# Causal attention between two expert layers: scores in sets of three heads over three PSUM banks, two sets in turn, and a probability ring of five

## The chip, the cores and the metric

The kernel runs on one NeuronCore of one Trainium2 chip. The metric is the device time of one execution in microseconds (us); the kernel before was timed three times.

## The reference

The input x has 2 sequences of 1024 tokens with 128 features. Three layers follow each other, each added to x: half of an expert layer, causal attention, and half of the same expert layer again.

```python
x = x + 0.5 * ffn(layernorm(x))     # 8 experts, 128 -> 256 -> 128, gelu, all summed, one gate value per token
x = x + attention(layernorm(x))     # 8 heads of 8 features
x = x + 0.5 * ffn(layernorm(x))
...
q, k = l2norm(q), l2norm(k)
sim = einsum('bhid,bhjd->bhij', q, k) * 8.0
attn = softmax(where(causal_mask, sim, finfo.min))
o = einsum('bhij,bhjd->bhid', attn, v) @ w_out
```

## The kernel before, in words

The program is written engine by engine. Each engine runs its own list in order, and every dependence is a semaphore: `scores_done`, `exp_done`, `mask_done` and `pv_done` count the four stages of attention.

**Expert layers.** Tokens go in four groups of 512; a group has 16 chunks of 128 hidden rows. A chunk is three matmuls up (`up`, L455), a gelu on ACT (L782), a split into a high and a low part on DVE (`split`, L949) and three matmuls down (`down`, L479). Attention lies between the last group of the first layer and the first group of the second.

**Attention.** The 8 heads form two quads of four. A pair is one sequence `b` and one group of 512 queries `qg`, with both quads; there are four pairs. A unit is one pair and one quad (L218). For each unit, `score_items` (L90) lists items: one per key block of 128 keys before the diagonal, then three for the four diagonal blocks, packed as 512 columns, 384 + 128 columns, and 256 columns. A unit with `qg` 0 has 3 items, one with `qg` 1 has 7. Before the change a whole unit is done before the next, so its sibling quad comes after it.

A step is one item of two heads; 80 steps make 40 quad steps. For a step:

- PE writes the scores of two heads into two banks of PSUM (`scores`, L592). Banks 0 to 5 form three sets (`S_SETS` = 3, `score_set`, L251), so scores of step s wait for the exponential of step s - 3 (`set_reader`, L255).
- ACT takes one exponential over both banks (`exp_scores`, L797) into a ring of 8 buffers (`P_SLOTS`). It waits for the probability product that last read the buffer.
- GpSimd (POOL) zeroes what lies above the diagonal with `affine_select` (L1305 to L1313), 128x256 elements each.
- PE multiplies the probabilities of four heads with v (`pv`, L606), in f32, into one output bank per pair (7 or 6 in turn), a row of 32 partitions per head.

The order on PE is written out at L685 to L713: for quad step k the two score sets, then `pv(k - 3)` (`PV_LAG` = 3), then perhaps one job.

Jobs (L242, `fill` L631 on PE, `empty` L1137 on DVE) use the other output bank: the layernorm transposes of the last token group ("ln"), its q, k, v product in two halves ("qkv"), the transposes of stacked q and k ("q_stack", "k_stack"), the output projection of a finished pair in two halves ("project") and the transposes for the second expert layer ("ffn_ln"). Each names the quad step whose `pv` it follows, counted from q1, q2, q3, the first quad steps of pairs 1 to 3. A job waits until DVE has emptied the job before it, and the first `pv` of pairs 2 and 3 waits for all jobs before it, since its output bank was the job bank.

```python
for k in range(quad_steps + PV_LAG):
    ...
        for s in (2 * k, 2 * k + 1):
            ...
            scores(s)
    ...
    if k >= PV_LAG:
        ...
        pv(k - PV_LAG)
        if jobs[next_job][0] == k - PV_LAG:
            fill(next_job)
```

Some steps are scored early, inside the last token group of the first expert layer (L537 to L557): steps 0 to 3, two on banks 0 and 1 and two on banks 2 and 3.

Of the kernel before, what the change touches and what calls it, by code (L numbers as in the profile page):

```python
# [48 lines left out]
QUADS = 2  # L49
ROW = 32  # L50
# [6 lines left out]
S_SETS = 3  # L57
P_SLOTS = 8
PV_LAG = 3
FFN, ATT = 0, 1  # L60
# [38 lines left out]
def build(nc, x, ln_w, ln_b, w_qkv, w_out, gate_w, gate_b, rms_w, w1, b1, w2, b2, out):  # L99
# [9 lines left out]
    with ctx:  # L109
        def sb(name, shape, dt=f32):  # L110
            return ctx.enter_context(nc.sbuf_tensor(name, shape, dt))
# [59 lines left out]
        probs = sb("probs", [P, P_SLOTS, 2, GROUP])  # L171
# [47 lines left out]
        steps = []  # L219
        for u, (b, qg, quad) in enumerate(units):  # L220
            items = score_items(qg)
            for k, item in enumerate(items):
                for pair in range(2):
                    steps.append(dict(unit=u, b=b, qg=qg, quad=quad, pair=pair, item=item, first=(k == 0),
                                      last=(k == len(items) - 1), local=k,
                                      diagonal=any(kt >= GROUP_TILES * qg for kt, *_ in item)))
        masks_until, n_masks = [], 0
        for st in steps:
            n_masks += len(st["item"]) if st["diagonal"] else 0
            masks_until.append(n_masks)  # L230
        quad_steps = len(steps) // 2
        quads_until_unit = [max(i for i, st in enumerate(steps) if st["unit"] == u) // 2 + 1 for u in range(len(units))]
        last_quad = [n - 1 for n in quads_until_unit]
# [5 lines left out]
        pairs = len(units) // QUADS  # L239
        first_of_pair = [0] + [quads_until_unit[QUADS * i - 1] for i in range(1, pairs)]  # L240
# [3 lines left out]
                (q1 + 12, "q_stack", LAST), (q2 + 1, "k_stack", LAST),  # L244
# [5 lines left out]

        def score_set(s):  # L251

            return s % 2 if s < 4 else (s - 2) % S_SETS

        def set_reader(s):  # L255

            return s - 2 if s in (2, 3) else None if s == 4 or s < 2 else s - S_SETS

        def output_bank(pair):
            return 7 - pair % 2  # L260

        def job_bank(n):

            at = jobs[n][0]
            return 13 - output_bank(steps[2 * min(at, quad_steps - 1)]["unit"] // QUADS)

        def pair_of_job(n):
            return steps[2 * min(jobs[n][0], quad_steps - 1)]["unit"] // QUADS
# [161 lines left out]
        def _(pe):  # L430
# [77 lines left out]
            def ffn_group(layer, g):  # L508
# [5 lines left out]
                for c in range(CHUNKS):  # L514
# [39 lines left out]
                    if operands and last and c >= at["att_qkv"]:  # L554
# [37 lines left out]
            def scores(s):  # L592
                st = steps[s]
                if set_reader(s) is not None:
                    pe.wait_ge(exp_done, set_reader(s) + 1)
                for kt, q0, width, at in st["item"]:
                    k0 = SEQ * st["b"] + P * kt
                    qc = SEQ * st["b"] + GROUP * st["qg"] + q0
                    for hd in range(2):
                        j = 2 * st["pair"] + hd  # L600
                        rows = slice(ROW * j, ROW * j + ROW)
                        m = pe.matmul(ps[:, 2 * score_set(s) + hd, at:at + width], kT[rows, st["quad"], k0:k0 + P],  # L602
                                      qT[rows, st["quad"], qc:qc + width], start=True, stop=True)
                m.then_inc(scores_done, 1)

            def pv(k):  # L606

                s = 2 * k
                st = steps[s]
                pair = st["unit"] // QUADS  # L610
                bank = output_bank(pair)
                opens, closes = st["first"] and st["quad"] == 0, st["last"] and st["quad"] == QUADS - 1
                if opens and pair == 0:
                    pe.wait_ge(kT_done, LAST - 1)
                if opens and pair == 1:
                    pe.wait_ge(resid, GROUP_TILES * GROUPS)
                if opens and pair > 1:
                    pe.wait_ge(job_emptied, sum(at < k for at, *_ in jobs))
                if st["diagonal"]:
                    pe.wait_ge(mask_done, masks_until[s + 1])  # L620
                else:
                    pe.wait_ge(exp_done, s + 2)
                for n, (kt, q0, width, at) in enumerate(st["item"]):
                    for j in range(4):
                        m = pe.matmul(ps[ROW * j:ROW * j + ROW, bank, q0:q0 + width],  # L625
                                      v_ones[:, SEQ // P * st["b"] + kt, 4 * st["quad"] + j, :],
                                      probs[:, (s + j // 2) % P_SLOTS, j % 2, at:at + width],
                                      start=(opens and n == 0), stop=(closes and n == len(st["item"]) - 1))
                m.then_inc(pv_done, 1)
# [54 lines left out]
            next_job = 0  # L684
            for k in range(quad_steps + PV_LAG):  # L685
                if k < quad_steps:
                    st = steps[2 * k]
                    if st["first"]:
                        p = Q_GROUPS * st["b"] + st["qg"]
                        if p < GROUPS // 2:  # L690
                            pe.wait_ge(kT_done, p + 1)
                        else:
                            pe.wait_ge(job_emptied, job_number["k_stack", p] + 1)
                    for s in (2 * k, 2 * k + 1):
                        if s < 4:
                            continue
                        if s == 4:
                            pe.wait_ge(qkv_copied, LAST)
                            pe.wait_ge(y_evac, GROUPS)
                            pe.wait_ge(xf_done[FFN], GROUPS)  # L700
                        scores(s)
                    if k == 0:
                        y_transposes(LAST, BANK_YT_LAST)
                if k >= PV_LAG:
                    if k == quad_steps + PV_LAG - 1:
# [20 lines left out]
        def _(act):  # L726
# [70 lines left out]
            def exp_scores(s):  # L797
                act.wait_ge(scores_done, s + 1)
# [76 lines left out]
            for s in range(2, len(steps)):  # L875
                exp_scores(s)
# [6 lines left out]
        def _(dve):  # L883
# [234 lines left out]
            def output(pair):  # L1118

                dve.wait_ge(pv_done, quads_until_unit[QUADS * pair + QUADS - 1])  # L1120
# [108 lines left out]
        def _(pool):  # L1229
# [75 lines left out]
            for s, st in enumerate(steps):  # L1305
                if not st["diagonal"]:
                    continue
                pool.wait_ge(exp_done, s + 1)

                for _, _, _, at in st["item"]:  # L1310
                    region = probs[:, s % P_SLOTS, :, at:at + P]
                    pool.affine_select(region, region, [[0, 2], [1, P]], ALU.is_ge, 0.0, base=0,  # L1312
                                       channel_multiplier=-1).then_inc(mask_done, 1)  # L1313
                if s == 5:
                    ln_twice(LAST)
                if s == 2 * last_quad[3] + 1:
                    ln_once(GROUPS)
# [20 lines left out]
```

## Time and profile before

| what | value |
|---|---|
| median of 3 runs | 288.85 us (288.41 to 289.15) |
| the profiled execution | 288.67 us, its span 286.9 us |
| PE busy | 274.2 us, 96% of the span |
| ACT busy | 222.8 us, 78% |
| DVE busy | 216.9 us, 76% |
| POOL busy | 87.6 us, 31% |
| granted TensorE clock, mean | 0.999 |

The span runs from the first to the last instruction; the execution's time holds 1.8 us more around it. Busy time of an engine is an average over stages: in the expert layers PE is busy throughout, while in attention, from 119 to 185 us, ACT has work almost all the time. A record of an operation may overlap the next, on PE and on ACT, so the pace of an engine is read from start to start, not from the length of a record. Where an engine idles, the page names the engine that ended the wait.

### The profile page before, as it was taken

The numbers are of one execution on the slowest core, as the hardware profiler recorded it, in microseconds if no ns is written. First come the engines' busy times: TensorE is split into PE (matmuls) and PEld (weight loads), VectorE is DVE, ScalarE is ACT, GpSimd is POOL, SyncE is SP. The second block draws the span as 40 slices with busy tenths as digits, with TensorE's granted clock in tenths as the row PEclk, the third lists the DMA queues.
The fourth block names the chain that finished last, engine by engine and source line by source line (L and its number), as shares of the span: only waits on it lengthen the run. The fifth ranks groups of instructions, "written<-read, shape, count | busy, mean of one in ns | idle before, by whom it ended". The sixth has DMA issues, their size and how long they took to land.

```text
span 286.9 us, 5191 instructions
## 1 busy us (share of the span) xinstructions
PE 274.2 (96%) x1651; PEld 191.6 (67%) x1651; DVE 216.9 (76%) x573; ACT 222.8 (78%) x346; POOL 87.6 (31%) x155
## 2 busy tenths in 40 slices
PE   8998999999989998899998999999999999999994
PEld 8675788788778886432433432378888888888882
DVE  7699989888989889855588153078788898797765
ACT  2766876868787785999999999976785877677672
POOL 6326203301890383361438321401300310310010
PEclk9999999999999999999999999999999999999999
DMA  5720000000000000000000000000001000100101
GB/s 156 233 73 1 0 1 2 0 0 1 2 1 0 3 1 0 0 2 2 0 3 0 3 0 2 0 2 0 0 2 39 0 0 0 37 0 2 38 0 37
DMA packets 8107, 4.64 MB, mean 16 GB/s; under 512 B 690, under 2 KB 8084, under 8 KB 8084
## 3 DMA queue, kind: packets, MB, share of 16 engines
q1 hardware_dynamic: 8084, 4.35, 5.3%
q8 instruction: 12, 0.20, 0.3%
q14 instruction: 11, 0.09, 0.1%
HBM read 3.30 MB, written 1.05 MB: 15 GB/s over the span
## 4 chain that ended last, share of the span: by engine, by line
PE 73%; POOL 8%; ACT 8%; issue 5%; DVE 4%; DVEq 0%; POOLq 0%; ACTq 0%
PE ps L494 9%; PE ps L489 9%; PE ps L471 8%; PE ps L477 8%; PE ps L474 8%; PE ps L492 8%; PE ps L625 8%; ACT probs L803 5%; PE ps L602 3%; PE ps L664 2%; PE ps L656 2%; PE ps L451 2%; PE ps L580 2%; PE ps L442 2%; POOL rstd L1231 1%
## 5 line engine op out<-in xcount | busy, mean ns | idle before, releaser
L790 ACT ACTIVATE h<-ps,cols 128x512 f32<-128x512 f32 x128 | 87.9, 691 | 48.8 <-PE ps L477 43.5
L958 DVE TENSOR_TENSOR h_lo<-h,h_hi 128x512 fp32r<-128x512 f32 x128 | 92.0, 724 | 29.6 <-ACT h_hi L793 27.1
L803 ACT ACTIVATE probs<-ps 128x1024 f32<-128x1024 f32 (+1 forms) x80 | 67.0, 1013 | 0.6 <-PE ps L602 0.4
L489 PE MATMUL ps<-h_hi,w_hi 128*128 128x512 f32 x128 | 52.9, 413 | 0.3 <-DVE h_hi L956 0.3
L494 PE MATMUL ps<-h_lo,w_hi 128*128 128x512 f32 x128 | 50.9, 398 | 1.4 <-DVE h_lo L958 1.4
L471 PE MATMUL ps<-xT_hi,w_hi 128*128 128x512 f32 (+1 forms) x128 | 50.7, 396 | 0.1
L477 PE MATMUL ps<-xT_lo,w_hi 128*128 128x512 f32 (+1 forms) x128 | 50.0, 391 | 0.0
L492 PE MATMUL ps<-h_hi,w_lo 128*128 128x512 f32 x128 | 50.0, 391 | 0.0
L474 PE MATMUL ps<-xT_hi,w_lo 128*128 128x512 f32 (+1 forms) x128 | 49.9, 389 | 0.0
L793 ACT ACTIVATE h_hi<-ps,cols 128x512 fp32r<-128x512 f32 x72 | 49.2, 683 | 0.0
L1312 POOL TENSOR_SCALAR_AFFINE_SELECT probs<-probs 128x256 f32<-128x256 f32 x64 | 26.0, 431 | 46.5 <-ACT probs L803 46.0
L625 PE MATMUL ps<-probs,v_ones 128*32 128x512 f32 (+3 forms) x384 | 38.8, 495 | 0.0
L494 PEld LDWEIGHTS ps<-h_lo,w_hi 128*128 128x128 f32 x128 | 24.0, 188 | 9.5 <-DVE h_lo L958 4.4
L956 DVE CAST h_hi<-h 128x512 fp32r<-128x512 f32 x56 | 24.9, 444 | 7.0 <-ACT h L790 6.2
L489 PEld LDWEIGHTS ps<-h_hi,w_hi 128*128 128x128 f32 x128 | 24.1, 188 | 5.8 <-DVE h_hi L956 1.6
L471 PEld LDWEIGHTS ps<-xT_hi,w_hi 128*128 128x128 f32 x128 | 24.0, 188 | 5.6 <-ACT h L790 0.4
L477 PEld LDWEIGHTS ps<-xT_lo,w_hi 128*128 128x128 f32 x128 | 24.0, 188 | 5.5 <-DVE xT_lo L1182 0.2
L474 PEld LDWEIGHTS ps<-xT_hi,w_lo 128*128 128x128 f32 x128 | 24.0, 188 | 5.1
L492 PEld LDWEIGHTS ps<-h_hi,w_lo 128*128 128x128 f32 x128 | 24.1, 189 | 3.9
L602 PE MATMUL ps<-qT,kT 32*128 32x512 f16 (+3 forms) x192 | 21.3, 329 | 2.9 <-ACT probs L803 2.3
L602 PEld LDWEIGHTS ps<-qT,kT 32*128 32x128 f16 x192 | 6.5, 91 | 25.2 <-ACT probs L803 15.1
L1231 POOL TENSOR_TENSOR gate_rms<-gate_ms,neg_half 128x4 f32<-128x4 f32 x8 | 10.6, 1320 | 28.5 <-DVE gate_ms L923 28.5
(130 smaller groups left out, 288.4 us busy)
## 6 DMA issues: line engine op xcount, KB each, us to landing
w_raw<-in_L_ffn_w SPq DMA_DIRECT2D x8, 256.0 KB, 4.9
x_sb<-in_L_attn_x SPq DMA_DIRECT2D x3, 256.0 KB, 6.8
out_x<-x_sb SPq DMA_DIRECT2D x3, 256.0 KB, 2.3
x_sb<-in_L_attn_x SPq DMA_DIRECT2D x2, 128.0 KB, 2.2
out_x<-x_sb SPq DMA_DIRECT2D x2, 128.0 KB, 1.8
wout_sb<-in_L_attn_w_out SPq DMA_DIRECT2D x8, 4.0 KB
wqkv_sb<-in_L_attn_w_qkv SPq DMA_DIRECT2D x1, 96.0 KB, 6.0
small<-in_L_ffn_b SPq DMA_DIRECT2D x1, 8.0 KB
```

Of the source, the lines that this page charges most:

```text
L471: pe.matmul(bank, w1_hi[:, w], xT_hi[:, cols_g], start=True, stop=False)
L474: pe.matmul(bank, w1_lo[:, w], xT_hi[:, cols_g], start=False, stop=False)
L477: pe.matmul(bank, w1_hi[:, w], xT_lo[:, cols_g], start=False, stop=True).then_inc(up_done, 1)
L489: pe.matmul(y, w2_hi[:, w], h_hi[:, c % RING, :], start=(c == 0), stop=False)
L492: pe.matmul(y, w2_lo[:, w], h_hi[:, c % RING, :], start=False, stop=False)
L494: pe.matmul(y, w2_hi[:, w], h_lo[:, c % RING, :], start=False, stop=(c == CHUNKS - 1)).then_inc(down_done, 1)
L602: m = pe.matmul(ps[:, 2 * score_set(s) + hd, at:at + width], kT[rows, st["quad"], k0:k0 + P], qT[rows, st["quad"], qc:qc + width], start=T ...
L625: m = pe.matmul(ps[ROW * j:ROW * j + ROW, bank, q0:q0 + width], v_ones[:, SEQ // P * st["b"] + kt, 4 * st["quad"] + j, :], probs[:, (s + j ...
L790: first = nc.scalar.activation(h[:, slot, :], ps[:, BANK_H + slot, :], ACT.Gelu, bias=bias)
L793: nc.scalar.activation(h_hi[:, slot, :], ps[:, BANK_H + slot, :], ACT.Gelu, bias=bias).then_inc(gelu_done, 1)
L803: nc.scalar.activation(probs[:, s % P_SLOTS, :, 0:width], ps[:, bank:bank + 2, 0:width], ACT.Exp, scale=SCALE).then_inc(exp_done, 1)
L958: dve.tensor_tensor(h_lo[:, slot, :], h[:, slot, :], h_hi[:, slot, :].bitcast(f32), ALU.subtract).then_inc(split_done, 1)
```

## The change

Slots take the place of steps of two heads. A slot is 512 columns of scores of one head; the 256-column items of both quads share a slot, so all 144 slots are full. The pairs go key block by key block, both quads of a key block after each other (`steps` is now one entry for four heads of one quad). Slots are cut into sets: three early sets of two, 45 sets of three, then two and one, 50 in all. From the fourth on a set has banks 0 to 2 or 3 to 5 in turn, so that scores of set n wait for the exponential of set n - 2. One exponential covers the whole set, up to 128x1536. The ring has five sets (`P_SETS`); the exponential of set n waits for all `pv` that read set n - 5. A `pv` comes on PE in the turn of set (its last set + 3), or + 4 where it is masked, after that set's scores. Masks take up to three slots at once. The job "k_stack" of the last group moves from the second quad step of pair 2 to the last of pair 1. Only three sets are scored early.

```diff
-S_SETS = 3
-P_SLOTS = 8
-PV_LAG = 3
+SET = 3
+P_SETS = 5
+EARLY_SETS = 3
+PV_LAG, PV_LAG_MASKED = 3, 4
...
+        sizes = [2] * EARLY_SETS
+        sizes += [SET] * ((len(slots) - sum(sizes)) // SET - 1) + [2, 1]
...
+        def set_bank(n):
+            return 2 * (n % 2) if n < EARLY_SETS else SET * (n % 2)
...
+        turn_of_step = [last_set[k] + (PV_LAG_MASKED if st["diagonal"] else PV_LAG) for k, st in enumerate(steps)]
+        turn_of_step = [max(turn_of_step[:k + 1]) for k in range(quad_steps)]
...
-                (q1 + 12, "q_stack", LAST), (q2 + 1, "k_stack", LAST),
+                (q1 + 12, "q_stack", LAST), (q1 + 13, "k_stack", LAST),
...
-            def scores(s):
-                st = steps[s]
-                if set_reader(s) is not None:
-                    pe.wait_ge(exp_done, set_reader(s) + 1)
+            def scores(n):
+                if banks_free_after(n):
+                    pe.wait_ge(exp_done, banks_free_after(n))
...
+            for n in range(EARLY_SETS, max(turn_of_step) + 1):
...
+                    scores(n)
+                while next_step < quad_steps and turn_of_step[next_step] == n:
+                    if next_step == quad_steps - QUADS:
+                        pe.wait_ge(exp_done, len(sizes) - 1)
                         for c in range(LAG):
-                            pe.wait_ge(exp_done, len(steps) - 2 + c // 2 + 1)
                             up(1, GROUPS, c, 0)
-                    pv(k - PV_LAG)
-                    if jobs[next_job][0] == k - PV_LAG:
+                    pv(next_step)
+                    if jobs[next_job][0] == next_step:
                         fill(next_job)
                         next_job += 1
+                    next_step += 1
...
-                if s >= P_SLOTS:
-                    act.wait_ge(pv_done, (s - P_SLOTS) // 2 + 1)
-                width = sum(w for _, _, w, _ in steps[s]["item"])
-                bank = 2 * score_set(s)
-                nc.scalar.activation(probs[:, s % P_SLOTS, :, 0:width], ps[:, bank:bank + 2, 0:width], ACT.Exp,
+                if n >= P_SETS:
+                    act.wait_ge(pv_done, max(steps_reading(n - P_SETS)) + 1)
+                bank = set_bank(n)
+                nc.scalar.activation(probs[:, n % P_SETS, 0:sizes[n], :], ps[:, bank:bank + sizes[n], :], ACT.Exp,
                                      scale=SCALE).then_inc(exp_done, 1)
```

The diff decides the order by these tables, so here is what PE's list becomes at two places. In it `ps<-qT,kT` is scores, `ps<-probs,v_ones` is `pv`, and `ps<-ident,q_stack` and `k_stack` are jobs. First PE where attention takes over, after the transposes of the last expert output; before, scores of steps 4 to 7 and then the first `pv`:

```order
L602 MATMUL ps<-qT,kT 128x256 [waits xf_done_ffn,y_evac,qkv_copied]
L602 MATMUL ps<-qT,kT 128x256
L602 MATMUL ps<-qT,kT 128x256 [waits exp_done]
L602 MATMUL ps<-qT,kT 128x256
L602 MATMUL ps<-qT,kT 128x512 [waits exp_done,kT_done]
L602 MATMUL ps<-qT,kT 128x512
L602 MATMUL ps<-qT,kT 128x512 [waits exp_done]
L602 MATMUL ps<-qT,kT 128x512
L625 MATMUL ps<-probs,v_ones 32x512 [waits mask_done,kT_done]
L625 MATMUL ps<-probs,v_ones 32x512 x3
```

Now, scores of sets 3, 4 and 5 and then the first `pv`:

```order
L650 MATMUL ps<-qT,kT 128x512 [waits xf_done_ffn,exp_done,y_evac,qkv_copied]
L650 MATMUL ps<-qT,kT 128x512
L650 MATMUL ps<-qT,kT 128x384
L650 MATMUL ps<-qT,kT 128x128
L650 MATMUL ps<-qT,kT 128x384 [waits exp_done]
L650 MATMUL ps<-qT,kT 128x384 x2
L650 MATMUL ps<-qT,kT 128x128 x3
L650 MATMUL ps<-qT,kT 128x384 [waits exp_done]
L650 MATMUL ps<-qT,kT 128x384 x2
L650 MATMUL ps<-qT,kT 128x128 x3
L673 MATMUL ps<-probs,v_ones 32x512 [waits mask_done,kT_done]
L673 MATMUL ps<-probs,v_ones 32x512 x3
```

The first `pv` stands behind scores that wait for an exponential two sets earlier; the exponential of set 5 in turn reuses the probabilities' buffer of set 0, which this `pv` reads.

Second PE at the seam from pair 1 to pair 2. Before, the q transposes of the last group follow one `pv`, scores follow them, then the `pv` of 256 columns and scores again; the k transposes come three quad steps after the q transposes, behind these rows:

```order
L580 MATMUL ps<-ident,q_stack 128x128 [waits stack_done,job_emptied]
L580 MATMUL ps<-ident,q_stack 128x128 x7
L602 MATMUL ps<-qT,kT 128x256 [waits exp_done]
L602 MATMUL ps<-qT,kT 128x256
L602 MATMUL ps<-qT,kT 128x256 [waits exp_done]
L602 MATMUL ps<-qT,kT 128x256
L625 MATMUL ps<-probs,v_ones 32x256 [waits mask_done]
L625 MATMUL ps<-probs,v_ones 32x256 x3
L602 MATMUL ps<-qT,kT 128x512 [waits exp_done,job_emptied]
L602 MATMUL ps<-qT,kT 128x512
L602 MATMUL ps<-qT,kT 128x512 [waits exp_done]
L602 MATMUL ps<-qT,kT 128x512
```

Now the two short steps of pair 1, with one job each, stand behind the scores of one set (set 28):

```order
L650 MATMUL ps<-qT,kT 128x384 [waits exp_done]
L650 MATMUL ps<-qT,kT 128x384 x2
L650 MATMUL ps<-qT,kT 128x128 x3
L673 MATMUL ps<-probs,v_ones 32x256 [waits mask_done]
L673 MATMUL ps<-probs,v_ones 32x256 x3
L623 MATMUL ps<-ident,q_stack 128x128 [waits stack_done,job_emptied]
L623 MATMUL ps<-ident,q_stack 128x128 x7
L673 MATMUL ps<-probs,v_ones 32x256 [waits mask_done]
L673 MATMUL ps<-probs,v_ones 32x256 x3
L623 MATMUL ps<-ident,k_stack 128x128 [waits stack_done,job_emptied]
L623 MATMUL ps<-ident,k_stack 128x128 x7
```

What moved: both `pv` of 256 columns and both transpose jobs are in one turn, between the scores of set 28 and those of set 29, the next rows.

## Rows read from the trace of the kernel before

**Rows 1.** The page: busy time of each engine and share of the span.
```profile
PE 274.2 (96%) x1651; PEld 191.6 (67%) x1651; DVE 216.9 (76%) x573; ACT 222.8 (78%) x346; POOL 87.6 (31%) x155
```

**Rows 2.** Busy time by stretch, attention: us, PE, PEld, DVE, ACT, POOL, PEclk, DMA, GB/s.
```profile
132.00:146.00 14.00, 14.00 (x136) 5.43 (x128) 8.85 (x27) 13.85 (x17) 3.75 (x8) 1.00 0.01 1
...
119.00:185.00 66.00, 61.77 (x620) 21.59 (x624) 34.63 (x99) 65.40 (x80) 27.05 (x66) 1.00 0.01 1
```

**Rows 3.** Groups by line and shape, 115 to 190 us: the exponentials.
```profile
L803 ACT ACTIVATE probs<-ps 128x1024 f32<-128x1024 f32 x64 | 59.9, 1099 | 0.2
...
L803 ACT ACTIVATE probs<-ps 128x512 f32<-128x512 f32 x16 | 9.2, 668 | 0.4 <-PE ps L602 0.4
```

**Rows 4.** Timeline, ACT alone: start us, us, engine, line, what.
```profile
119.15 1.02 ACT L803 ACTIVATE probs<-ps 128x1024 f32<-128x1024 f32 x1
...
172.74 1.02 ACT L803 ACTIVATE probs<-ps 128x1024 f32<-128x1024 f32 x1
...
183.60 1.22 ACT L803 ACTIVATE probs<-ps 128x512 f32<-128x512 f32 x2
...
184.08 0.74 ACT L803 ACTIVATE probs<-ps 128x512 f32<-128x512 f32 x1
```

**Rows 5.** Timeline, PE: scores, probs times v, and jobs, back to back.
```profile
132.65 0.66 PE L647 MATMUL ps<-ident,xn 128*128 128x128 f32 x4
...
142.97 0.92 PE L650 MATMUL ps<-wqkv_sb,xf 128*128 128x192 f32 x4
...
143.82 0.40 PE L602 MATMUL ps<-qT,kT 32*128 32x512 f16 x4
...
144.14 1.07 PE L625 MATMUL ps<-probs,v_ones 128*32 128x512 f32 x8
...
145.14 0.62 PE L580 MATMUL ps<-ident,q_stack 128*128 128x128 f16 x8
...
145.69 0.40 PE L602 MATMUL ps<-qT,kT 32*128 32x512 f16 x4
...
154.63 0.29 PE L602 MATMUL ps<-qT,kT 32*128 32x256 f16 x4
...
154.85 0.64 PE L625 MATMUL ps<-probs,v_ones 128*32 128x256 f32 x8
...
162.98 0.71 PE L656 MATMUL ps<-wout_sb,o_feat 128*128 128x128 f32 x4
```

**Rows 6.** Timeline, PE: scores that ACT waits for, and scores that wait for ACT.
```profile
172.31 0.40 PE L602 MATMUL ps<-qT,kT 32*128 32x512 f16 x4
...
177.48 0.39 PE L602 MATMUL ps<-qT,kT 32*128 32x512 f16 x2 [0.47 <-ACT probs L803]
```

**Rows 7.** The chain that ended last, 171 to 186 us.
```profile
176.37 0.40 ACT probs L803
...
179.99 0.79 ACT probs L803
```

**Rows 8.** Timeline, DVE and PE: a job that waits, and one emptied.
```profile
153.32 0.62 DVE L378 TENSOR_TENSOR k_stack<-qkn,k_stack 128x256 f16<-128x256 f32 x1
...
154.09 0.61 PE L580 MATMUL ps<-ident,q_stack 128*128 128x128 f16 x8 [0.81 <-DVE k_stack L378]
...
163.72 0.42 DVE L1170 TENSOR_TENSOR x_sb<-ps,x_sb 128x256 f32<-128x256 f32 x1 [4.04 <-PE ps L656]
```

**Rows 9.** Timeline, POOL: masks.
```profile
171.75 1.48 POOL L1312 TENSOR_SCALAR_AFFINE_SELECT probs<-probs 128x256 f32<-128x256 f32 x4 [0.15 <-ACT probs L803]
...
181.16 0.41 POOL L1312 TENSOR_SCALAR_AFFINE_SELECT probs<-probs 128x256 f32<-128x256 f32 x1 [7.92 <-ACT probs L803]
```

**Rows 10.** Timeline, PE: start of the exponential stream and its end.
```profile
120.06 0.44 PE L602 MATMUL ps<-qT,kT 32*128 32x256 f16 x4
...
185.91 0.50 PE L471 MATMUL ps<-xT_hi,w_hi 128*128 128x512 f32 x1
...
188.75 0.50 PE L471 MATMUL ps<-xT_hi,w_hi 128*128 128x512 f32 x1
```

More of the change, by code:

```diff
@@ L218, in build @@
         units = [(b, qg, quad) for b in range(BATCH) for qg in range(Q_GROUPS) for quad in range(QUADS)]
-        steps = []
-        for u, (b, qg, quad) in enumerate(units):
+        pairs = len(units) // QUADS
+        slots, steps = [], []
+        for pair in range(pairs):
+            b, qg, _ = units[QUADS * pair]
             items = score_items(qg)
             for k, item in enumerate(items):
[L223 to L226, printed above, removed]
+                width = sum(w for _, _, w, _ in item)
+                together = width < GROUP
+                diagonal = any(kt >= GROUP_TILES * qg for kt, *_ in item)
+                first_slot = len(slots)
+                for quads in ([range(QUADS)] if together else [[quad] for quad in range(QUADS)]):
+                    for j in range(4):
+                        slots.append(dict(pair=pair, b=b, qg=qg, item=item, diagonal=diagonal, j=j, opens=(k == 0),
+                                          heads=[(quad, width * n) for n, quad in enumerate(quads)]))
+                for quad in range(QUADS):
+                    steps.append(dict(pair=pair, b=b, quad=quad, item=item, diagonal=diagonal,
+                                      slot=first_slot if together else first_slot + 4 * quad,
+                                      base=width * quad if together else 0,
+                                      opens=(k == 0 and quad == 0),
+                                      closes=(k == len(items) - 1 and quad == QUADS - 1)))
@@ new lines, in banks_free_after, with steps_reading, mask_regions @@
+        def banks_free_after(n):
+            mine = range(set_bank(n), set_bank(n) + sizes[n])
+            users = [m for m in range(n) if any(bank in mine for bank in range(set_bank(m), set_bank(m) + sizes[m]))]
+            return max(users) + 1 if users else 0
+        def steps_reading(n):
+            return [k for k, st in enumerate(steps) if any(set_of_slot[st["slot"] + j] == n for j in range(4))]
+        def mask_regions(n):
+            regions = []
+            for i, slot in enumerate(slots_of[n]):
+                if not slots[slot]["diagonal"]:
+                    continue
+                starts = sorted(at + base for _, base in slots[slot]["heads"] for *_, at in slots[slot]["item"])
+                if regions and regions[-1][2] == starts and regions[-1][1] == i:
+                    regions[-1][1] = i + 1
+                else:
+                    regions.append([i, i + 1, starts])
+            return regions
@@ L234, in build @@
+        turn_of_step = [last_set[k] + (PV_LAG_MASKED if st["diagonal"] else PV_LAG) for k, st in enumerate(steps)]
+        turn_of_step = [max(turn_of_step[:k + 1]) for k in range(quad_steps)]
+        steps_until_pair = [sum(st["pair"] <= pair for st in steps) for pair in range(pairs)]
+        last_mask_of_pair = [max(n for n in range(len(sizes)) if any(slots[i]["pair"] == pair and slots[i]["diagonal"] for i in slots_of[n]))
+                             for pair in range(pairs)]
         halves = ((0, 1), (2, 3))
@@ L235, in build @@
         SEED_OPS = 4
[L239 to L240 removed]
+        first_of_pair = [0] + steps_until_pair[:-1]
         q1, q2, q3 = first_of_pair[1:]
@@ L590, in stack_transposes @@
                 transpose_stack(k_stack, BANK_KT).then_inc(stack_t, 1)
-            def scores(s):
-                st = steps[s]
-                if set_reader(s) is not None:
-                    pe.wait_ge(exp_done, set_reader(s) + 1)
[L596 to L603, printed above, removed]
+            def scores(n):
+                if banks_free_after(n):
+                    pe.wait_ge(exp_done, banks_free_after(n))
+                parts = max(len(slots[i]["item"]) * len(slots[i]["heads"]) for i in slots_of[n])
+                for part in range(parts):
+                    for i in slots_of[n]:
+                        slot = slots[i]
+                        pieces = [(quad, base, piece) for quad, base in slot["heads"] for piece in slot["item"]]
+                        if part >= len(pieces):
+                            continue
+                        quad, base, (kt, q0, width, at) = pieces[part]
+                        k0 = SEQ * slot["b"] + P * kt
+                        qc = SEQ * slot["b"] + GROUP * slot["qg"] + q0
+                        rows = slice(ROW * slot["j"], ROW * slot["j"] + ROW)
+                        bank = set_bank(n) + i - first_slot[n]
+                        m = pe.matmul(ps[:, bank, base + at:base + at + width], kT[rows, quad, k0:k0 + P],
+                                      qT[rows, quad, qc:qc + width], start=True, stop=True)
@@ L604, in scores @@
                 m.then_inc(scores_done, 1)
             def pv(k):
-                s = 2 * k
-                st = steps[s]
-                pair = st["unit"] // QUADS
+                st = steps[k]
+                pair = st["pair"]
                 bank = output_bank(pair)
-                opens, closes = st["first"] and st["quad"] == 0, st["last"] and st["quad"] == QUADS - 1
-                if opens and pair == 0:
+                if st["opens"] and pair == 0:
                     pe.wait_ge(kT_done, LAST - 1)
-                if opens and pair == 1:
+                if st["opens"] and pair == 1:
@@ L683, in _ @@
             pe.wait_ge(wout_in, 16 * HEADS)
[L684 to L705, printed above, removed]
+            y_transposes(LAST, BANK_YT_LAST)
@@ L874, in _ @@
             ffn_groups(nc.scalar, 0, lambda g: ffn_group(0, g))
-            for s in range(2, len(steps)):
-                exp_scores(s)
+            for n in range(2, len(sizes)):
+                exp_scores(n)
             for c in range(LAG):
```

75 lines of the change are left out of this document (45 added, 30 removed).

## Prediction

> **What bounds the kernel now.** I read the page first, then the busy time by stretch, then the timeline of each engine inside attention. The page gives PE 96% of the span [rows 1], and the expert layers, which the change leaves alone, make that share. Attention is the stretch from 119 to 185 us: ACT is busy for 65.4 of 66.0 us, PE for 61.8 [rows 2]. Between 132 and 146 us PE is busy for all of 14.0 us [rows 2]. So the reader should see two engines that are both nearly full: ACT sets the pace, and PE has next to nothing to spare where jobs lie between the steps.
>
> ACT's own pace is read from starts. From 172.74 to 183.60 us twelve exponentials of 1024 columns begin, 0.905 us each; the last two, of 512 columns, begin 0.48 us apart [rows 4]. A column thus costs (0.905 - 0.48) / 512 = 0.83 ns and an instruction 0.055 us on top. There are 64 and 16 of them [rows 3]; two ran before 119.15 us. The rest need 62 x 0.905 + 15 x 0.48 = 63.3 us up to the start of the last, which came 64.9 us after 119.15 [rows 4]: ACT lost only 1.6 us to waits. The three sets of banks keep it fed.
>
> **What the change gives.** Columns stay the same: 144 slots of 512, or 64 x 1024 + 16 x 512. Instructions go from 80 to 50, which saves 30 x 0.055 = 1.65 us if ACT never waits. A set of 1536 columns should take 0.48 + 2 x 0.425 = 1.33 us; no row has that width, and I extend the line through the two that are there.
>
> The row leaves 0.055 us for an instruction. [...]
>
> **What it costs: the loop of two sets.** Steps on the loop, each from a row. Scores that wait for ACT start 1.11 us after the start of a 0.905 us exponential (176.37 [rows 7] to 177.48 [rows 6]), so 0.21 after its pace is over. Four heads' scores occupy PE for 0.33 us (145.69 to the next piece; 143.82 to 144.14 gives 0.32) [rows 5], and I take that for three. From the start of scores to the start of the waiting exponential is 0.43 (172.31 [rows 6] to 172.74 [rows 4]), so 0.10 for the signal. A `pv` of 512 columns takes 1.00 (144.14 to 145.14 [rows 5]); one of 256 takes 0.57, its record of 0.64 running 0.07 into the next as the others do [rows 5]. By the same reading jobs take 0.59 (ln), 0.85 (half of qkv), 0.55 (a stack) and 0.64 (half a projection) [rows 5]. Between a job's end and PE's next job DVE needs 0.10 to start, 0.42 to add (162.98 + 0.64 to 163.72) and 0.15 back to PE (153.94 to 154.09) [rows 5, 8], about 0.69.
>
> Call the start of exponential n - 2 zero. Exponential n is due at 2.66. Its banks are free at 1.33 + 0.21 = 1.54, its scores end at 1.87, ACT could go at 1.97. Before, the banks of step s were those of s - 3 and scores ran a set ahead. Now PE has, after the scores of set n, until 3.99 - 0.43 = 3.56 for all other work of that turn without hurting set n + 1: 1.69 us. One `pv` and a projection (1.64) just fit; more does not, and a second such turn has only 1.00.
>
> 1. *Start.* The third early set has banks 0 and 1, so set 3 needs banks that the last expert output holds. Its scores can start where those of step 4 now do, 120.06 [rows 10]; add 0.43: 120.49, against 119.15 + 0.905 = 120.05. Loss 0.44. Before, steps 2 and 3 covered this.
> 2. *The ring of five.* In masked stretches `pv` comes with a lag of four sets, so the exponential of set n waits for a `pv` that PE does after the scores of set n itself: 1.87 + 1.00 + 0.10 = 2.97 against 2.66, 0.30 each. A late set gives the next one room, so it is paid at about every second set. Going through the 50 sets with these numbers I find it at sets 5, 7, 10, 23, 26, 30, 32, 34 and 47: 9 x 0.30 = 2.70. After set 23 a stack job lies between, and set 24 pays 0.55.
> 3. *Seam of pairs 0 and 1* (turn 11): `pv` 0.57 + 0.57 + 1.00, ln 0.59 = 2.73, less 1.69, less 0.30 already late: 0.74.
> 4. *qkv jobs* (turns 18 and 19): 1.85 each, so 0.16, then 1.85 - 1.00 = 0.85, together 1.01.
> 5. *Projections* of pairs 0 and 2, two turns in a row: 2 x 1.64 - 1.69 - 1.00 = 0.59, less about 0.3 since the turn before them is empty: 2 x 0.3 = 0.6.
> 6. *Seam of pairs 1 and 2* (turn 28): exponential 28 waits for the second short `pv`, behind a stack: 1.87 + 0.57 + 0.55 + 0.57 + 0.10 = 3.66, loss 1.00. The second stack then waits for DVE in the shadow of that.
> 7. *Seam of pairs 2 and 3* (turn 35): exponential 35 waits for `pv` 0.57, projection 0.64, `pv` 0.57: 3.75 - 2.66 - 0.30 = 0.79. Then the second projection waits 0.12 for DVE and takes 0.64, the first `pv` of pair 3 waits 0.69 for its output bank and takes 1.00, and only then come the scores of set 36, 0.43: 2.88, less 0.10 and 1.33 that set 35 covers: 1.45.
>
> Sum of waits: 0.44 + 2.70 + 0.55 + 0.74 + 1.01 + 0.60 + 1.00 + 2.24 = 9.28 us, in place of 1.6.
>
> *The end.* Before, from the end of the last exponential's pace (184.08 + 0.48) to PE's free run into the second expert layer (188.75 [rows 10]) are 4.19 us. Now from the start of set 47: 1.33, POOL's start 0.27 (179.99 + 0.905 to 181.16 [rows 7, 9]), four masks of about 0.37 or less, 1.22 together [rows 9], about 0.2 back to PE (my estimate, beside the 0.15 from DVE), `pv` 1.0, three chunks up 2.27 (185.91 to 188.75 less a `pv` of 0.57 [rows 5, 10]), two short `pv` 1.14: 7.43, while ACT ends at 1.33 + 0.905 + 0.48 = 2.71. So 4.72, a loss of 0.53.
>
> Costed at nothing: the masks elsewhere (POOL is busy for 27 of 66 us [rows 2] and has four sets of time), and the moved "k_stack" beyond point 6. If that cover goes, see the third rival. No DMA is moved in attention.
>
> **Sum.** 9.28 - 1.6 - 1.65 + 0.53 = +6.6 us on the profiled execution's own 288.67 us: 295.2; the median of the runs lies 0.18 us higher, so 295.4 us. The unknown prices are the hand-overs between PE and ACT, met some ten times on the path. 0.1 us more or less on each moves 1.0 us. Scores of a set cost between 0.22, what four heads of 256 columns take (154.63 to 154.85 [rows 5]), and 0.33; the nearest row has 512 columns as the sets do, so 0.33; the lower end takes 2 us off. ACT's line could be steeper over a third bank: 0.05 us a set would add 2. The forecast's own range is 292.8 to 298.
>
> **Rivals.**
> - *Faster: ACT never waits.* If PE's part of the two-set loop took 1.33 us or less instead of 0.21 + 0.33 + 1.00 + 0.10 = 1.64, the ring would not bind, and with PE ahead the seams would shrink to what they cost before: 288.85 - 1.65 = 287.2, or down to 285.6 if the old 1.6 us of waits went too. For it: ACT is the fuller engine by [rows 2]. Against: the `pv` alone is 1.00 and its order behind the scores is written out. The Trainium skill (Perfetto Trace Analysis, Optimizing Scalar/DVE Operations) says that grouping into larger operations can raise throughput where the engine is saturated; by that rule the result is this rival's 287.2, and rows 2 bear out the saturation, but not that the fuller engine stays fed with two sets. Chance 0.07.
> - *Half hidden.* The seams cost, the ring does not (`pv` done just in time): less 2.70 and 0.55, 292.2. No row shows ACT waiting for the ring before. Chance 0.10, with another 0.05 that more is hidden and the time comes out within 0.3% of before.
> - *Worse: DVE or POOL late too.* At turn 28 the stacked q and k must be ready; DVE's chain from the second qkv half to them took from 143.82 [rows 5] to 153.94 [rows 8], 10.1 us, with PE waiting 0.81 for it; nine sets between those jobs now give 12.0 us. With 1 us of delay there and masks late by 0.2 at ten places: 298.4. A drop of TensorE's clock in the new gaps is part of it; it was granted in full, the level of 2.4 GHz, in all of attention [rows 2]. Chance 0.10.
> - That the change does not do what it says is excluded by the order of the lists.
>
> **How the numbers follow.** Forecast 0.68, worse 0.10, half hidden 0.10, within bounds of no change 0.05, faster 0.07. 0.3%, 0.9 us, is about what a measurement of this kernel can tell from no change. So slower 0.88, same 0.05, faster 0.07. The range leaves out the faster rival, no change and the far end of the worse one: 292.0 to 298.5.
>
> **What would show it.** Exponentials of 1536 columns 1.33 us apart in the full stretches of pairs 1 and 3, and 1.6 apart at about every second set in masked ones; gaps on ACT of 1 us at the first quad step of pairs 2 and 3; the waits for PE behind ACT grown from 0.4 us to some 9. Wrong if ACT stays busy for 98% of attention, if its gaps end at POOL, or if a set of three takes clearly more than 1.33 us.

## The result and the profile after

The changed kernel takes 297.4 us (median of 4 runs, 297.23 to 300.49), beside 288.77 us before: 1.0325 times the time before, 95% interval 1.0297 to 1.0352. The ratio goes by the mean of the runs, which the one of 300.49 us raises (its clock was granted at 0.971 on the mean, beside 0.981 to 0.985 in the others); the medians alone give 1.030. The forecast was 295.4 us, the range 292.0 to 298.5, and slower was the likeliest side. The profiled execution took 297.23 us with a span of 295.5 us, 8.56 us more than the profiled one before; the difference below is between these two.

The page of the changed kernel, busy time and the clock granted in 40 slices of the span:

```profile
PE 274.9 (93%) x1651; PEld 190.6 (65%) x1651; DVE 216.4 (73%) x573; ACT 222.9 (75%) x316; POOL 86.2 (29%) x150
...
PEclk9999999999999999779999999999999999999998
```

Hardly any engine does more than in [rows 1]: PE 0.7 us, ACT 0.1, the others less than before. The span grew by 8.6 us, so what grew is waiting. Two slices of the clock read 7, where attention begins.

Busy time by stretch in the changed kernel, all of attention and then a piece of pair 3 (columns as in rows 2):

```profile
119.00:193.00 74.00, 62.37 (x614) 20.40 (x614) 33.95 (x99) 65.11 (x49) 24.87 (x58) 0.95 0.01 1
176.00:189.00 13.00, 11.40 (x103) 3.43 (x99) 3.95 (x9) 13.00 (x11) 1.75 (x4) 1.00 0.00 1
```

ACT was busy for 65.40 of 66.0 us [rows 2]; now it is for 65.11 of 74.0. In pair 3 it is still full. Which engine ended its idle time, in the groups by line and shape (115 to 194 us), and then in the view of waits (119 to 193 us: total us, times, longest us):

```profile
L846 ACT ACTIVATE probs<-ps 128x1536 f32<-128x1536 f32 x45 | 62.6, 1455 | 8.9 <-PE ps L673 6.2 <-PE ps L650 2.5
```

```profile
ACT probs L846 <- PE ps L673: 6.2, 12, 1.4
ACT probs L846 <- PE ps L650: 2.5, 5, 1.0
```

Before, the exponentials waited 0.6 us [rows 3]; now 8.9, of which 8.7 are put down to PE. 6.2 us in 12 waits end at L673: the exponential waits for a `pv` that must empty its buffer of the ring. Five waits end at L650, late scores: the first at the start of the stream, the other four behind jobs.

The changed kernel's timeline, ACT alone; a number in brackets is the idle time before a row, so every row is a new stretch after a wait:

```profile
119.11 1.02 ACT L846 ACTIVATE probs<-ps 128x1024 f32<-128x1024 f32 x1
120.48 2.79 ACT L846 ACTIVATE probs<-ps 128x1536 f32<-128x1536 f32 x2 [0.35 <-PE ps L650]
124.30 2.79 ACT L846 ACTIVATE probs<-ps 128x1536 f32<-128x1536 f32 x2 [1.03 <-PE ps L673]
128.50 1.45 ACT L846 ACTIVATE probs<-ps 128x1536 f32<-128x1536 f32 x1 [1.41 <-PE ps L673]
130.22 2.79 ACT L846 ACTIVATE probs<-ps 128x1536 f32<-128x1536 f32 x2 [0.27 <-PE ps L673]
133.25 2.79 ACT L846 ACTIVATE probs<-ps 128x1536 f32<-128x1536 f32 x2 [0.23 <-PE ps L673]
136.33 4.13 ACT L846 ACTIVATE probs<-ps 128x1536 f32<-128x1536 f32 x3 [0.29 <-PE ps L650]
...
157.60 2.79 ACT L846 ACTIVATE probs<-ps 128x1536 f32<-128x1536 f32 x2 [0.32 <-PE ps L673]
161.32 2.79 ACT L846 ACTIVATE probs<-ps 128x1536 f32<-128x1536 f32 x2 [0.92 <-PE ps L673]
...
170.39 1.45 ACT L846 ACTIVATE probs<-ps 128x1536 f32<-128x1536 f32 x1 [0.23 <-PE ps L673]
172.51 1.45 ACT L846 ACTIVATE probs<-ps 128x1536 f32<-128x1536 f32 x1 [0.67 <-PE ps L673]
175.00 14.99 ACT L846 ACTIVATE probs<-ps 128x1536 f32<-128x1536 f32 x11 [1.03 <-PE ps L650]
190.21 2.86 ACT L846 ACTIVATE probs<-ps 128x1536 f32<-128x1536 f32 x3 [0.23 <-PE ps L673]
```

How to read a loss from it: a row of three lasts 4.13 us, the last record of 1.45 included, so two steps of 1536 columns take 2.68, or 1.33 to 1.34 each. Two rows begin 3.82 us apart (120.48, 124.30) with two exponentials in the first: 3.82 - 2.66 = 1.16 us lost before the second. Summed over all rows, ACT loses 11.7 us from 119.11 to the start of its last exponential at 192.47, 73.36 us later. Before, those 64.93 us held 1.63 us of losses [rows 4]. So +10.0 of losses, -1.6 for the exponentials saved, and the tail adds 0.18: from 192.47 + 0.48 to PE's free run (197.32, the last row below) are 4.37 us instead of 4.19 [rows 10]. Together 8.6, as measured.

The changed kernel's timeline, PE, where the stream opens, and where it ends:

```profile
119.47 0.63 PE L548 MATMUL ps<-ident,yT 128*128 128x128 f32 x4 [0.98 <-ACT yT L856]
120.03 0.61 PE L650 MATMUL ps<-qT,kT 32*128 32x512 f16 x10
121.98 0.39 PE L650 MATMUL ps<-qT,kT 32*128 32x384 f16 x6 [1.34 <-ACT probs L846]
122.31 1.88 PE L673 MATMUL ps<-probs,v_ones 128*32 128x512 f32 x8
...
197.32 0.50 PE L514 MATMUL ps<-xT_hi,w_hi 128*128 128x512 f32 x1
```

The first `pv` lasts 1.88 us here and 1.07 in [rows 5]. The clock tells why. Busy time by stretch, first before, then after:

```profile
120.00:122.40 2.40, 1.67 (x16) 0.56 (x16) 2.16 (x10) 2.40 (x5) 2.02 (x6) 1.00 0.00 0
122.40:129.30 6.90, 6.51 (x78) 2.03 (x70) 3.70 (x17) 6.90 (x10) 4.57 (x11) 1.00 0.01 2
```

```profile
120.00:122.40 2.40, 1.05 (x21) 0.50 (x24) 2.19 (x11) 2.05 (x3) 0.81 (x3) 1.00 0.00 0
122.40:129.30 6.90, 5.74 (x34) 0.86 (x38) 3.87 (x16) 4.46 (x4) 5.06 (x13) 0.51 0.01 2
```

PE worked 1.05 of the 2.40 us from 120.00 on, with one wait of 1.34 us in them and one of 0.98 us before 119.47. Before the change it had worked 1.67, and its two waits there were 0.72 and 0.66 us. Then its clock was granted at 0.51, the level of 1.2 GHz, for 6.9 us, and two of the largest losses of ACT, at sets 5 and 7 (1.16 and 1.54 us), lie there.

### The profile page after: what moved, and what is told of

The parts are those of the page before. It is cut to its first block, busy times and chain, and to the rows that moved or that the text cites. A ratio compares the mean times of both kernels' runs of the same rounds, so it can differ in the third digit from the quotient of the medians.

```text
span 295.5 us, 5127 instructions
## 1 busy us (share of the span) xinstructions
PE 274.9 (93%) x1651; PEld 190.6 (65%) x1651; DVE 216.4 (73%) x573; ACT 222.9 (75%) x316; POOL 86.2 (29%) x150
## 3 DMA queue, kind: packets, MB, share of 16 engines
HBM read 3.30 MB, written 1.05 MB: 15 GB/s over the span
## 4 chain that ended last, share of the span: by engine, by line
PE 73%; ACT 10%; POOL 8%; issue 4%; DVE 3%; DVEq 0%; ACTq 0%; POOLq 0%
PE ps L673 9%; PE ps L537 9%; PE ps L532 8%; PE ps L514 8%; PE ps L520 8%; PE ps L517 8%; PE ps L535 8%; ACT probs L846 8%; PE ps L650 4%; PE ps L712 2%; PE ps L704 2%; PE ps L494 2%; PE ps L485 1%; POOL rstd L1274 1%; PE ps L613 1%
## 5 line engine op out<-in xcount | busy, mean ns | idle before, releaser
L846 ACT ACTIVATE probs<-ps 128x1536 f32<-128x1536 f32 (+2 forms) x50 | 67.0, 1403 | 8.9 <-PE ps L673 6.2
L1355 POOL TENSOR_SCALAR_AFFINE_SELECT probs<-probs 128x384 f32<-128x384 f32 (+2 forms) x59 | 24.6, 443 | 56.7 <-ACT probs L846 56.7
L673 PE MATMUL ps<-probs,v_ones 128*32 128x512 f32 (+3 forms) x384 | 40.4, 515 | 0.5 <-DVE x_sb L1213 0.5
L650 PE MATMUL ps<-qT,kT 32*128 32x512 f16 (+3 forms) x192 | 19.5, 339 | 10.3 <-ACT probs L846 10.2
L650 PEld LDWEIGHTS ps<-qT,kT 32*128 32x128 f16 x192 | 5.3, 92 | 31.6 <-ACT probs L846 21.1
```

What stands on the lines that cost most here:

```text
L650: m = pe.matmul(ps[:, bank, base + at:base + at + width], kT[rows, quad, k0:k0 + P], qT[rows, quad, qc:qc + width], start=True, stop=True)
L846: nc.scalar.activation(probs[:, n % P_SETS, 0:sizes[n], :], ps[:, bank:bank + sizes[n], :], ACT.Exp, scale=SCALE).then_inc(exp_done, 1)
```

## The experiments

The theory: with sets of three only two fit into six banks, so the time from an exponential to the scores in its banks, and from a `pv` to the exponential in its ring buffer, is on the path. The rivals: the lower clock alone, the order by key block or the full slots themselves, and the places of the jobs.

**The clock.** Matmuls of ones against ones, whose output nobody reads, stand before the scores of sets 5, 7 and 10: 8, 8 and 5 calls, the bank being one that is free then.

```diff
+            def keep_warm(n):
+                bank = 7 if n == 5 else 6
+                if n > 5:
+                    pe.wait_ge(resid, GROUP_TILES * GROUPS)
+                for _ in range(5 if n == 10 else 8):
+                    pe.matmul(ps[:, bank, 0:P], ones[:, :], ones[:, :], start=True, stop=True)
...
+                    if n in (5, 7, 10):
+                        keep_warm(n)
                     scores(n)
```

> The changed kernel with 21 idle 128x128 matmuls of ones on TensorE, eight before the scores of set 5, eight before set 7, five before set 10, where TensorE waits anyway; they write a bank that nobody uses then. Theory (the half clock from 122.4 to 129.3 us comes from TensorE's idleness at the opening of attention): the clock stays at its full level there, the waits before sets 5, 7 and 8 fall from 3.1 to some 0.6 us, and the time from 297.4 to about 295.0 us. Rival (the drop has nothing to do with idleness): the clock falls as before, 297.4 us or a little more.

It took 296.18 us (4 runs), 1.025 (1.0222 to 1.0278) of before, 1.2 more than expected. The clock stayed at full speed, but the timeline of PE in this run shows what the fill cost:

```profile
120.59 2.05 PE L719 MATMUL ps<-ones 128*128 128x128 f32 x16
122.57 0.39 PE L650 MATMUL ps<-qT,kT 32*128 32x384 f16 x6
```

Eight calls make 16 records and take 2.05 us, so the scores of set 5 begin at 122.57, not at 121.98. Half as many were tried next: 4, 4 and 2 calls, `range(2 if n == 10 else 4)`.

> As the kernel with 21 idle matmuls, with half as many: four before set 5, four before set 7, two before set 10. The 21 held the clock but took 0.25 us each and delayed the scores of sets 5, 7 and 10 by 0.6, 0.65 and 0.4 us. Theory: four fit the gap, the clock stays full, ACT loses 0.3 us at each of sets 5, 7 and 10, and the time is 297.4 - 2.5 = 294.9 us. Rival (four are too few): the clock falls again, 297.4 us.

It took 294.7 us (4 runs), 1.0193 (1.017 to 1.0217), as expected. Its busy time by stretch, and its timeline of ACT there:

```profile
120.00:122.40 2.40, 2.14 (x25) 1.48 (x26) 1.99 (x9) 2.05 (x3) 0.56 (x2) 1.00 0.00 0
122.40:129.30 6.90, 6.33 (x67) 2.67 (x61) 4.32 (x18) 6.44 (x5) 5.93 (x15) 1.00 0.01 2
```

```profile
120.73 2.79 ACT L855 ACTIVATE probs<-ps 128x1536 f32<-128x1536 f32 x2 [0.35 <-PE ps L650]
123.75 2.79 ACT L855 ACTIVATE probs<-ps 128x1536 f32<-128x1536 f32 x2 [0.23 <-PE ps L673]
126.78 4.14 ACT L855 ACTIVATE probs<-ps 128x1536 f32<-128x1536 f32 x3 [0.23 <-PE ps L673]
```

With the clock held, sets 5 and 7 lose 3.02 - 2.66 = 0.36 and 3.03 - 2.66 = 0.37 us, set 8 nothing. In the changed kernel these three lost 1.16, 1.54 and 0.39, 3.09 in all. The lower clock is thus 2.4 us of ACT's waits, and 2.7 us of the medians (297.4 - 294.7). It is real and it is the smaller part: 5.6 us remain over the 289.07 us that the kernel before took beside this run. Were the clock alone the cause, the whole loss would have gone.

**The ring.** One buffer more, `P_SETS = 6` for 5.

> The changed kernel with six sets in the probability ring instead of five, nothing else. Theory (the ring binds only in masked stretches, and TensorE's crowded turns at the seams of pairs bind behind it): the waits of some 0.3 us for pv vanish, the seams grow by part of that, 1.9 us off: 295.5 us. Rival 1 (the ring is most of the loss): 4 us or more off, 293.4 or below. Rival 2 (the ring is only where TensorE's lateness shows): no change, 297.4.

It took 293.7 us (4 runs), 1.016 (1.013 to 1.019), 1.8 less than expected. It lies next to the 293.4 of the first rival and not at the theory's 295.5: the ring alone is 3.7 of the 8.6 us. No exponential waits for `pv` any more; from its timeline of ACT, the two longest waits that remain:

```profile
161.12 9.51 ACT L846 ACTIVATE probs<-ps 128x1536 f32<-128x1536 f32 x7 [2.04 <-PE ps L650]
...
172.78 17.74 ACT L846 ACTIVATE probs<-ps 128x1536 f32<-128x1536 f32 x14 [2.15 <-PE ps L650]
```

These stand at the two seams, 1/2 and 2/3, where points 6 and 7 had forecast 1.00 us, and 2.24 in two parts. With the ring loose ACT runs further ahead into them, and PE's order decides. The clock fell here too: it was granted at 0.54 from 122.4 to 129.3 us.

**The lag.** `pv` of masked steps a turn earlier, `PV_LAG_MASKED = 3` for 4; the ring then binds by one set less.

> The changed kernel with the masked pv in the turn of its last set + 3 instead of + 4, nothing else. Theory: the ring no longer binds, and the short steps of a pair are spread over two turns: 3.8 us off, 293.6 us; less if the half clock stays. Rival (GpSimd's masks come too late for a lag of three): waits of TensorE for masks take the place, 297 us or more.

It took 291.6 us (4 runs), 1.0101 (1.0069 to 1.0133), 2.0 less than expected. PE has the first `pv` earlier, and the clock did not fall in the opening; this run's stretch there, then its timeline of ACT from the start, and of PE and ACT at the seam 1/2:

```profile
120.00:122.40 2.40, 1.80 (x24) 0.41 (x20) 2.33 (x13) 2.15 (x2) 1.01 (x4) 1.00 0.02 7
```

```profile
120.25 16.23 ACT L846 ACTIVATE probs<-ps 128x1536 f32<-128x1536 f32 x12 [0.35 <-PE ps L650]
...
155.59 0.61 PE L623 MATMUL ps<-ident,q_stack 128*128 128x128 f16 x8 [1.85 <-DVE k_stack L421]
...
157.98 9.51 ACT L846 ACTIVATE probs<-ps 128x1536 f32<-128x1536 f32 x7 [2.64 <-PE ps L650]
```

The ring's waits are gone with one constant: twelve exponentials of 1536 columns run without a wait from 120.25 us, still with two sets in turn, where the changed kernel waited five times. But the seam has grown to one wait of 2.64 us: PE now stands 1.85 us for DVE's stacks, and the scores behind that job are late. That is the wait for DVE, at the same job, that the third rival described. The two short steps are not spread over two turns, as the expectation had it: both stand with both stack jobs before the scores of set 28. Why PE waits shows in DVE's chain from the second qkv half to the stacks, from the timelines of DVE and PE, first in the changed kernel, then in this run:

```profile
147.91 0.42 DVE L1198 COPY qk_raw<-ps 128x256 f32<-128x256 f32 x1 [1.48 <-PE ps L698]
158.79 0.74 DVE L421 TENSOR_TENSOR k_stack<-qkn,k_stack 128x256 f16<-128x256 f32 x1
160.00 0.62 PE L623 MATMUL ps<-ident,q_stack 128*128 128x128 f16 x8
```

```profile
144.15 0.42 DVE L1198 COPY qk_raw<-ps 128x256 f32<-128x256 f32 x1 [1.48 <-PE ps L698]
154.71 0.73 DVE L421 TENSOR_TENSOR k_stack<-qkn,k_stack 128x256 f16<-128x256 f32 x1
```

DVE needs about as long in both, 11.6 us (147.91 to 159.53) and 11.3 (144.15 to 155.44). PE came to the job 12.1 us after the start of the chain in the changed kernel and 9.6 us after it here (155.59 - 1.85 = 153.74): with a lag shorter by a turn and without the ring's waits, PE is there too soon.

**Width and order apart.** All of the change but the width: sets of two heads in three places in turn, as before, with the same key-block order and 512 columns in every slot. The ring has 8 sets of two.

```diff
-SET = 3
-P_SETS = 5
-EARLY_SETS = 3
-PV_LAG, PV_LAG_MASKED = 3, 4
+SET = 2
+P_SETS = 8
+EARLY_SETS = 4
+PV_LAG, PV_LAG_MASKED = 5, 5
...
-        sizes = [2] * EARLY_SETS
-        sizes += [SET] * ((len(slots) - sum(sizes)) // SET - 1) + [2, 1]
+        sizes = [SET] * (len(slots) // SET)
...
-            return 2 * (n % 2) if n < EARLY_SETS else SET * (n % 2)
+            return SET * (n % 2) if n < EARLY_SETS else SET * ((n - 2) % 3)
...
-                        pe.wait_ge(exp_done, len(sizes) - 1)
                         for c in range(LAG):
+                            pe.wait_ge(exp_done, len(sizes) - 1 + (c < 2))
```

> The changed kernel's order of slots (key block by key block, both quads, all slots full) with the scores back in sets of two heads, three sets in turn and a ring of eight; 72 exponentials of 1024 columns. Theory (two sets in turn are what costs): no half clock, ACT's waits some 4 us instead of 11.6, 290.6 us, between the two kernels and nearer to the one before. Rival (the new order with its two short steps and their jobs at each seam is most of the loss): 294 us or more. Other rival (only the 0.055 us per exponential counts once there are three sets): 288.3 us.

It took 288.69 us (10 runs), 0.9989 (0.9977 to 1.0000): no difference from before that can be measured, and 1.9 less than expected, next to the 288.3 of the other rival. Its timeline of ACT:

```profile
118.89 24.85 ACT L845 ACTIVATE probs<-ps 128x1024 f32<-128x1024 f32 x27
143.97 11.20 ACT L845 ACTIVATE probs<-ps 128x1024 f32<-128x1024 f32 x12 [0.23 <-PE ps L649]
156.36 9.29 ACT L845 ACTIVATE probs<-ps 128x1024 f32<-128x1024 f32 x10 [1.18 <-PE ps L649]
166.15 19.37 ACT L845 ACTIVATE probs<-ps 128x1024 f32<-128x1024 f32 x21 [0.50 <-PE ps L649]
```

27 exponentials run without a wait where the changed kernel waited seven times. So neither the order by key block nor the full slots cost anything that shows in the time: the whole loss goes with the sets of three. But the width went and so did the number of sets in turn, the ring's length and the lags. The next run parts the first two: the same kernel with two sets in turn, in four banks.

```diff
-            return SET * (n % 2) if n < EARLY_SETS else SET * ((n - 2) % 3)
+            return SET * (n % 2)
...
-                            pe.wait_ge(exp_done, len(sizes) - 1 + (c < 2))
+                            pe.wait_ge(exp_done, len(sizes) - (c < 2))
```

> Sets of two heads as in the level kernel, but only two sets in turn (banks 0 to 3), ring of eight and all else the same: one wait changed, from the exponential three sets before to two sets before. Theory (what costs is that scores wait for the exponential two sets before, with all other work of TensorE between): 288.7 + 4.4 = 293.1 us. Rival (what costs is the width of three heads): 288.7 us.

It took 296.46 us (4 runs), 1.0258 (1.023 to 1.0286): 7.8 us over the run with three in turn, where 4.4 was expected. Width, order, ring and lags are the same in both. Their views of waits, first with three sets in turn, then with two:

```profile
ACT probs L845 <- PE ps L649: 1.9, 3, 1.2
```

```profile
ACT probs L845 <- PE ps L649: 6.3, 10, 1.5
```

The clock was full in both, and no exponential waits for `pv`: ten waits for scores that began late. So two sets in turn cost 7.8 us with two heads. With three heads the price hung on ring and lag: 8.7 us over the run with three sets of two in turn as the change stands (297.4), 5.0 with a sixth ring set (293.7), 2.9 with the short lag (291.6). Why the reckoning was short by 3.4 us was not followed further; 6.3 of the 7.3 us between the two profiled runs lie in the stream of exponentials, which takes 72.9 us here (119.24 to 192.15) and 66.6 with three sets in turn (118.89 to 185.52), the rest before and behind it.

**The jobs.** If in the run with two heads the waits left stand at jobs (1.18 and 0.50 above), jobs elsewhere should end them: the last k stack to the first quad step of pair 2, the projection of pair 1 a quad step earlier.

```diff
-                (q1 + 12, "q_stack", LAST), (q1 + 13, "k_stack", LAST),
-                (q2 + 4, "project", (1, 0)), (q2 + 5, "project", (1, 1)),
+                (q1 + 12, "q_stack", LAST), (q2, "k_stack", LAST),
+                (q2 + 3, "project", (1, 0)), (q2 + 4, "project", (1, 1)),
```

> Sets of two heads, three in turn, as in the kernel that came out level with the one before, and three jobs moved: the last k_stack one step later, to the first of pair 2, the projection of pair 1 one step earlier, so that no two jobs and short steps meet at a seam. That kernel lost 1.4 us at set 41 and 0.7 at set 51. Theory (jobs in crowded turns are what is left): ACT's waits fall from 3.1 to some 1.6 us, 287.2 us, faster than both kernels. Rival (the k transposes come too late for pair 3, or DVE is the one that is late): 288.7 us or more.

It took 287.52 us (6 runs, 287.05 to 287.75), 0.9949 (0.9932 to 0.9966): 1.5 us less than before, and faster than both kernels. Its timeline of ACT:

```profile
118.73 24.85 ACT L845 ACTIVATE probs<-ps 128x1024 f32<-128x1024 f32 x27
143.81 40.03 ACT L845 ACTIVATE probs<-ps 128x1024 f32<-128x1024 f32 x43 [0.23 <-PE ps L649]
```

70 exponentials with one wait that the view shows; the rest of what is lost is in pauses too short for it. The same move with three heads and the short lag (k stack at `q2`, projections at `q2 + 2` and `q2 + 3`):

> Sets of three heads with a masked lag of three, and the last k_stack one step later, the projection of pair 1 two steps earlier. With the lag alone set 28 lost 2.8 us, where TensorE waited 1.85 for DVE's stacks, and set 35 lost 0.8. Theory: 0.7 to 1 us off, 290.8 us; the rest of the distance to the kernel before is the loop of two sets. Rival (sets of three can be had without loss once the jobs lie well): 289 us or less.

It took 291.57 us (4 runs), 1.0078 (1.0052 to 1.0103), the same as without the move, a miss. Its timeline of PE, and its busy time by stretch just behind:

```profile
156.08 0.61 PE L623 MATMUL ps<-ident,q_stack 128*128 128x128 f16 x8 [1.85 <-DVE k_stack L421]
```

```profile
157.00:160.60 3.60, 3.60 (x35) 1.26 (x28) 2.52 (x5) 2.79 (x2) 1.00 (x2) 0.54 0.00 0
```

PE still waits 1.85 us for DVE, at the q stack, which the move left in its place. Behind that wait the clock fell to 0.54 for 3.6 us, and ACT's losses are 6.3 us as without the move: the waits of 2.64 and 0.64 us have become 1.94, 0.74, 0.49 and 0.39. The fall of the clock goes into that, so the run doesn't tell what the move is worth by itself. Whether any version with three heads reaches the time before stays open: none here did.

## Why the prediction was right

The forecast was 2.0 us low, its side and its mechanism held. Losses of ACT by the prediction's points, from starts in the timeline of ACT as above, in us:

| point | forecast | measured |
|---|---|---|
| 1, start (set 3) | 0.44 | 0.47 |
| 2, ring at sets 5, 7 (and 8) | 0.60 | 3.09 |
| 2, ring at the other sets, with the second projections | 2.40 | 2.85 |
| 2, set 24 behind a stack | 0.55 | 0.55 |
| 3, seam 0/1 | 0.74 | 0.42 |
| 4, qkv jobs | 1.01 | 0.97 |
| 5, first projections | 0.30 | 0.31 |
| 6, seam 1/2 | 1.00 | 1.06 |
| 7, seam 2/3 | 2.24 | 1.95 |
| sum | 9.28 | 11.67 |

**The loop of two sets** held, with the ring of five and the lag of four that it was reckoned for. Sums of PE's pieces from rows before gave 0.30 at about every second masked set, and ACT lost time at all nine sets that the prediction named; the rows of 130.22 and 133.25, with the clock back, and the run with the clock held show 0.36 to 0.37. All of ACT's waits end at PE's lines, none at POOL, which the prediction had named as the sign of its failure. The exponentials of 1536 columns come 1.33 to 1.34 us apart, where the line through two widths gave 1.33; 30 instructions saved are worth about the 1.65 us that were forecast.

**The seams** held in place and nearly in size. Points 3 and 7 were too dear by 0.3 each, as was the end (0.18 in place of 0.53; its 1.22 for four masks isn't in [rows 9], which show 1.48). Together 1.0 us too much.

**The step that failed** is the ring's price at its first sets: "nine times 0.30" takes `pv` at 1.00 us everywhere, and the prediction kept a fall of TensorE's clock for a part of its third rival, with no price of its own. It fell where the ring binds first, and `pv` took 1.88. With the run that holds the clock in place of sets 5 to 8 the sum is 11.67 - 3.09 + 0.73 = 9.31, beside 9.28. The forecast was thus right but for the clock, and part of its agreement comes from terms that were off by some tenths both ways.

**The rivals.** "ACT never waits" is excluded by 8.9 us of waits: ACT stayed saturated only from 176 to 189 us and in a few shorter stretches, not where `pv` is masked. "Half hidden" fell with 12 waits at L673. Of the third rival, the clock fell, but POOL and DVE were not late in the changed kernel: no wait of PE ended at POOL, and two at DVE, of 0.5 and 0.2 us, both already in points 6 and 7. DVE was late, by 1.85 us, once the lag was shortened.

The Trainium skill (Perfetto Trace Analysis, Optimization Strategy) says that bubbles which come regularly can mean too few buffers in SBUF or PSUM; the trace agrees, with a wait at about every second masked set. Both kinds of buffer count here: a sixth set in the ring, which lies in SBUF, took 3.7 us off (293.7), and the pair of runs with two and three PSUM sets in turn (296.46 and 288.69 us) shows the other.

## What to carry to other kernels

Before widening an instruction to save its fixed cost, count how many sets of buffers are left in turn: here 30 x 0.055 us were saved and 10 us of waits bought. Most of the waits (6.2 of 8.9 us) came from an exponential needing a `pv` that PE does behind scores which themselves wait for an exponential: hand-over, scores and `pv` (1.64 us) don't fit beside one exponential (1.33 us). A sixth buffer or a `pv` one turn earlier took those waits away, so set ring and lag anew when the number of sets changes. Read the saving from starts of two widths and the price from the work of the other engine that stands between a buffer's release and its next use. When the waits are gone, move the jobs that remain away from the points where a pair begins and ends: that gave 1.2 us with two heads, and nothing with three, where DVE was late.

## What the runs showed of the hardware

The clock fell after an opening in which no wait of PE was longer than 1.34 us; PE had worked 1.05 of the 2.40 us before. With 2.14 (filled) and 1.80 (short lag) of 2.40 it stayed at full speed; before the change, 1.67. Then it kept the 1.2 GHz level for 6.9 us, in which PE was busy for 5.74. Holding it gave 2.7 us back, more than the 1.65 us of all the exponentials saved. In the run with three heads and moved jobs it fell after one wait of 1.85 us; PE was then busy for all of the 3.60 us that followed, at 0.54. The run with the short lag alone had the same wait of 1.85 us and kept the full clock, as its busy time by stretch shows:

```profile
157.00:160.60 3.60, 3.33 (x42) 1.14 (x42) 2.80 (x5) 2.62 (x2) 1.10 (x2) 1.00 0.00 0
```

So the length of a wait alone doesn't tell here whether the clock falls.

A matmul of 128 columns in f32, 128 by 128, makes two records and takes 0.25 us a call (120.59 to 122.57 for 8), so eight overfill a wait of 1.34 us and four don't.
